# Turning the attention's output by transposing transfers in place of TensorE

## What is computed

```python
x = x + attention(group_norm(x))      # layer 0
x = x + factorised(group_norm(x))     # layer 1
# attention: f = Wq x + bq, g = Wk x + bk (32 channels each), h = Wv x + bv (256)
#   s = f^T g (4096 x 4096 an image); beta = softmax(s, axis=1); o = gamma * h beta
# factorised: y = relu(bn(w1 x + b1)) (32 channels); all 528 products y_i * y_j;
#   z = relu(bn(w2 products + b2)) (256)
```

## Time and profile before

| what | value |
|---|---|
| median of 3 runs | 2105.32 us (2105.01 to 2105.93) |
| the profiled execution, time and span | 2109.38 us, 2107.6 us |
| granted TensorE clock | full speed in every slice |
| DMA, mean share of the 16 engines | 66.6% for the one queue of SyncE |
| transposes by TensorE, `tps<-idn,ot` | 256 |

### The profile page before, as it was taken

The page is one execution under the profiler, slowest core; times in us unless marked ns, Lnnn a source line. Parts: engine busy times, 40 slices in busy tenths (PEclk is TensorE's granted clock), DMA queues, the critical chain, the costliest instruction groups (busy, mean ns, idle before and its releaser), DMA issues.

```text
span 2107.6 us, 48084 instructions
## 1 busy us (share of the span) xinstructions
PE 2056.0 (98%) x17334; PEld 1611.1 (76%) x17334; DVE 1656.5 (79%) x3617; ACT 1539.2 (73%) x2456; POOL 1479.8 (70%) x2110
## 2 busy tenths in 40 slices
PE   5899999999999999999999999999999999999999
PEld 3688888888877777777877777777787777777854
DVE  8788988778777877878768788777877768777767
ACT  5677777767776777778777787777777777777767
POOL 3265666667677777878768787777867767677766
PEclk9999999999999999999999999999999999999999
DMA  5165778776476788778478678887836767675632
GB/s 190 37 101 103 129 143 143 139 132 113 84 133 122 146 158 150 154 145 156 98 140 140 117 156 142 159 167 139 157 78 134 144 124 140 118 142 94 139 72 81
DMA packets 728269, 271.89 MB, mean 129 GB/s; under 512 B 674240, under 2 KB 681152, under 8 KB 728000
## 3 DMA queue, kind: packets, MB, share of 16 engines
q1 hardware_dynamic: 728032, 268.82, 66.6%
HBM read 77.07 MB, written 19.92 MB: 46 GB/s over the span
## 4 chain that ended last, share of the span: by engine, by line
PE 86%; DVE 5%; POOL 3%; ACT 2%; issue 2%; DMA 1%; SPq 0%; DVEq 0%; ACTq 0%; POOLq 0%
PE acc L1784 19%; PE acc L1772 19%; PE acc L1773 18%; PE tps L1577 5%; PE acc L1577 5%; PE sps L1597 4%; PE acc L1571 3%; PE tps L1648 3%; PE tps L1650 2%; PE acc L1648 1%; POOL kb L1162 1%; PE tps L1612 1%; DVE ks L863 1%; PE tps L1634 1%; POOL xl L1139 1%
## 5 line engine op out<-in xcount | busy, mean ns | idle before, releaser
L1162 POOL TENSOR_TENSOR kb<-ks,kb 128x512 f16<-128x512 f32 x630 | 760.3, 1211 | 412.1 <-DVE kb L891 315.6
L1772 PE MATMUL acc<-hth,kt 128*128 128x257 f16 x2520 | 587.2, 273 | 1.1 <-DMA kt<-kb 1.1
L1773 PE MATMUL acc<-htl,kt 128*128 128x256 f16 x2520 | 586.6, 273 | 0.0
L1333 ACT ACTIVATE ph<-sps,esc 128x512 f16<-128x512 f32 x394 | 269.5, 684 | 339.7 <-PE sps L1597 329.8
L1345 ACT ACTIVATE ks<-ks,kbias,esc 128x512 f32<-128x512 f32 x630 | 498.9, 805 | 0.0
L1784 PE MATMUL acc<-hth,kt 128*128 128x257 f16 x2520 | 385.8, 274 | 0.0
L863 DVE TENSOR_SCALAR_CACHE_REDUCE ks<-acc 128x512 f32<-128x512 f32 x378 | 259.2, 686 | 158.8 <-PE acc L1577 157.0
L1772 PE MATMUL acc<-hth,ph 128*128 128x257 f16 x1576 | 367.3, 274 | 0.0
L1773 PE MATMUL acc<-htl,ph 128*128 128x256 f16 x1576 | 366.9, 273 | 0.0
L1784 PEld LDWEIGHTS acc<-hth,kt 128*128 128x128 f16 x2520 | 247.7, 98 | 100.6
L1772 PEld LDWEIGHTS acc<-hth,kt 128*128 128x128 f16 x2520 | 247.0, 98 | 41.6 <-issue 6.2
(11 more groups left out here) (254 smaller groups left out, 3444.7 us busy)
## 6 DMA issues: line engine op xcount, KB each, us to landing
rt<-turned SPq DMA_DIRECT2D x96, 256.0 KB, 4.9
xt<-x SPq DMA_DIRECT2D x46, 512.0 KB, 4.5
xb<-x SPq DMA_DIRECT2D x32, 512.0 KB, 4.7
out<-zt SPq DMA_DIRECT2D x45, 256.0 KB, 2.7
kt<-kb SPq DMA_TRANSPOSE x630, 3.2
yb<-turned SPq DMA_DIRECT2D x36, 128.0 KB, 2.6
rt<-turned SPq DMA_DIRECT2D x72, 64.0 KB, 2.2
turned<-yb SPq DMA_DIRECT2D x12, 256.0 KB, 2.5
```

Of the source, the lines that this page charges most:

```text
L1162: tt(kb[:, m % KB_RING, 1], ks[:, m % KS_RING], kb[:, m % KB_RING, 0], ALU.subtract).then_inc(kl_ok, 1)
L1333: A(ph[:, v % SLOTS], sps[v % 2][:], ACT.Exp, scale=esc[:]).then_inc(ph_ok, 1)
L1772: mm(bank[:, 0:C + 1], high[:, q], hth[:, c * QT + q], start=(s8 == 0 and q == 0), stop=False)
L1773: mm(bank[:, 0:C], high[:, q], htl[:, c * QT + q], start=False, stop=False)
```

## The change

The outputs of the chunks J = 0 to 6 of each image (28 of 32, `by_transfer`) are turned by a transposing transfer. ScalarE divides into a float16 high half (`oth[:, k, 0]`, the same memory as `ot`); VectorE takes the low half from PSUM at s8 = 5 of the next tile (`output_low`); SyncE turns both halves of one tile into a new buffer `od` in one transfer (`turn_output`, s8 = 7, 128 x 512 float16). In the next chunk VectorE adds the high half and then the low half, each times the output scale, to x (`finish_turned`, four instructions of 128 x 512 at t = 9, 10, 12 and 14), and takes the statistics at t = 16 and 17 (`own_stats`). TensorE's transposes at t = 4 and 7 are gone, and the waits that stood with them are at t = 9; the last chunk of an image is turned by TensorE as before. The ring of x has 13 slots in place of 14, which gives the room for `od`, so that seven more x chunks pass through `xt`. The order of the value chunks, and the steps of four of them and of three statistics, are moved.

```diff
-XR = 14
+XR = 13
+        od = sb("od", [P, QT, 2 * H2, P], f16)
+        oth = ot[:].rearrange("p t c -> p (t c)").bitcast(f16).rearrange("p (t e c) -> p t e c", t=QT, e=2)
-        VORD = (4, 0, 5, 1, 6, 2, 3, 7)
+        VORD = (4, 0, 5, 3, 6, 1, 2, 7)
-        LATER_STATS = ((2, 27), (3, 2), (3, 9), (3, 18), (3, 25), (4, 2), (4, 9), (4, 18), (4, 25), (5, 2), (5, 9), (5, 18),
+        LATER_STATS = ((2, 27), (3, 2), (3, 11), (3, 18), (3, 25), (4, 2), (4, 11), (4, 18), (4, 25), (5, 2), (5, 11), (5, 18),
                        (6, 22), (6, 29), (7, 4), (7, 11))
-        V_EARLY = (12, 15, 18, 21)
+        V_EARLY = (11, 15, 19, 26)
         def in_place(b, c):
-            return b == 0 or (c < XR - NCH if b == 1 else c < 4)
+            return b == 0 or (c < XR - NCH if b == 1 else c < 3)
+        def by_transfer(G):
+            return G % NCH != NCH - 1
+        def transfers_before(G):
+            return G - G // NCH
+        def tiles_lowered(tile):
+            return QT * transfers_before(tile // QT) + (tile % QT + 1 if by_transfer(tile // QT) else 0)
...
+            def turn_output(tile):
+                G, k = divmod(tile, QT)
+                sp.wait_ge(ot_low, tiles_lowered(tile))
+                if transfers_before(G):
+                    sp.wait_ge(own_ok, 2 * H2 * transfers_before(G))
+                sp.dma_start_transpose(od[:, k], oth[:, k].rearrange("p e c -> p (e c)")).then_inc(od_in, 16)
...
+                        if t % NCH == 7 and tile and by_transfer((tile - 1) // QT) and (J or t >= NCH):
+                            turn_output(tile - 1)
...
+            def output_low(tile):
+                k = tile % QT
+                dve.wait_ge(ot_act, tile + 1)
+                V.scalar_tensor_tensor(oth[:, k, 1], acc[tile % 2][:, 0:C], rinv[:, k:k + 1], oth[:, k, 0],
+                                       ALU.mult, ALU.subtract).then_inc(ot_low, 1)
+            def finish_turned(G, e, h):
+                b, J = divmod(G, NCH)
+                if e == h == 0:
+                    dve.wait_ge(od_in, 16 * QT * (transfers_before(G) + 1))
+                    dve.wait_ge(bv_ok, G + 1)
+                if e:
+                    dve.wait_ge(own_ok, 2 * H2 * transfers_before(G) + h + 1)
+                own = xb[:, x_slot(b, J), h].rearrange("p (t q) -> p t q", t=QT)
+                V.scalar_tensor_tensor(own, od[:, :, H2 * e + h], vout[:, h:h + 1], own,
+                                       ALU.mult, ALU.add).then_inc(own_ok, 1)
+            def own_stats(G, h):
+                b, J = divmod(G, NCH)
+                dve.wait_ge(own_ok, 2 * H2 * transfers_before(G) + H2 + h + 1)
+                V.bn_stats(bst[:, h, J], xb[:, x_slot(b, J), h])
...
+                        if s8 == 5 and tile and by_transfer((tile - 1) // QT) and (J or t >= NCH):
+                            output_low(tile - 1)
...
-                        if J and t in (5, 8):
-                            finish(G - 1, (t - 5) // 3, 1)
-                        if J and t in (6, 11):
-                            second_stats(G - 1, (t - 6) // 5, 1)
+                        if J and t in (9, 10, 12, 14):
+                            finish_turned(G - 1, *((0, 0), (0, 1), (1, 0), (1, 1))[(9, 10, 12, 14).index(t)])
+                        if J and t in (16, 17):
+                            own_stats(G - 1, t - 16)
...
+                if transfers_before(G):
+                    act.wait_ge(od_in, 16 * QT * transfers_before(G))
+                if by_transfer(G):
+                    A(oth[:, k, 0], acc[tile % 2][:, 0:C], ACT.Copy, scale=rinv[:, k:k + 1]).then_inc(ot_act, 1)
+                    return
...
-                        if J and t in (4, 7):
-                            if t == 4 and b and n >= 1:
+                        if J and t == 9:
+                            if b and n >= 1:
                                 pe.wait_ge(y_ok, y_made(n - 1))
...
-                            transposed(G - 1, (t - 4) // 3, 1)
...
                         elif s8 == 0 and tile >= 2:
                             pe.wait_ge(ot_act, tile - 1)
+                            if by_transfer((tile - 2) // QT):
+                                pe.wait_ge(ot_low, tiles_lowered(tile - 2))
```

More of the change, by code:

```diff
@@ L203, in build @@
         rinv_ok = sem("rinv_ok")
-        ot_act = sem("ot_act")
+        ot_act, ot_low, od_in, own_ok = sem("ot_act"), sem("ot_low"), sem("od_in"), sem("own_ok")
         y_mm, y_ok = sem("y_mm"), sem("y_ok")
@@ L1051, in attend @@
                             normed(("qk", b + 1, 2 * (J - 2)))
-                        if b < LASTB and J == NCH - 1 and t in (13, 16, 19, 22):
-                            normed(("v", b + 1, VORD[(13, 16, 19, 22).index(t)]))
+                        if b < LASTB and J == NCH - 1 and t - 1 in V_EARLY:
+                            normed(("v", b + 1, VORD[V_EARLY.index(t - 1)]))
             project()
@@ L1225, in _ @@
                             low(("qk", b + 1, 2 * (J - 3) + 1))
-                        if t in (14, 17, 20, 23) and b < LASTB and J == NCH - 1:
-                            low(("v", b + 1, VORD[(14, 17, 20, 23).index(t)]))
+                        if t - 2 in V_EARLY and b < LASTB and J == NCH - 1:
+                            low(("v", b + 1, VORD[V_EARLY.index(t - 2)]))
                         if t == 20 and b and 1 <= n < SHARED - 1:
@@ L1349, in divide @@
                 act.wait_ge(rinv_ok, tile + 1)
-                k = tile % QT
+                k, G = tile % QT, tile // QT
+                if transfers_before(G):
[3 more added lines that the diff above has]
+                    return
                 A(ot[:, k], acc[tile % 2][:, 0:C], ACT.Copy, scale=rinv[:, k:k + 1]).then_inc(ot_act, 1)
@@ L1456, in attend @@
                             high(("qk", b + 1, 2 * (J - 2)))
-                        if b < LASTB and J == NCH - 1 and t in (12, 15, 18, 21):
-                            high(("v", b + 1, VORD[(12, 15, 18, 21).index(t)]))
+                        if b < LASTB and J == NCH - 1 and t in V_EARLY:
+                            high(("v", b + 1, VORD[V_EARLY.index(t)]))
             act.wait_ge(set_dve, mark["scaled_qkv"])
@@ L1747, in attend @@
                             rest_of_z(n - 2)
-                        if J and t in (4, 7):
-                            if t == 4 and b and n >= 1:
+                        if J and t == 9:
+                            if b and n >= 1:
                                 pe.wait_ge(y_ok, y_made(n - 1))
-                            if t == 4 and b and n >= 2:
+                            if b and n >= 2:
                                 pe.wait_ge(z_ok, 2 * (n - 1))
-                            if t == 4 and b < LASTB and 4 <= J <= 7:
+                            if b < LASTB and 4 <= J <= 7:
                                 pe.wait_ge(qk_lo, qk_made(b + 1, 2 * (J - 4)))
-                            if (b, J, t) == (0, 2, 4):
+                            if (b, J) == (0, 2):
                                 pe.wait_ge(set_dve, mark["part1"])
-                            transposed(G - 1, (t - 4) // 3, 1)
                         if kept(u):
```

## The result

The changed kernel takes 2168.98 us (2166.16 to 2170.22), the kernel before 2105.62 (2105.01 to 2109.87) beside it: a ratio of 1.0294, with a 95% interval of 1.0278 to 1.0311. It is 63 us slower. I had forecast 9 us slower, with a range up to 2132. Every ratio here has an interval of some 0.15% (3 us) on either side, so a difference between two changed kernels is known to about 4 us.

A forecast was written before the change was run, and what follows sets the result against it. TensorE was taken to bound the kernel (busy 2056.0 of 2107.6 us). 2109.4 - 24.6 (transposes) + 36.9 (VectorE's backlog) - 3 (relief) = 2118.7; with the runs' median 4.1 lower, 2115 us, range 2088 to 2132.

The forecast's parts named there:

- VectorE's backlog: VectorE running behind TensorE, mainly t = 9 to 18; added work makes TensorE wait: 36.9 us, less 3 us relief elsewhere.
- Image 0: Its chunks lose most: 2.3 us each for J = 3 to 6, 3.6 each for J = 1, 2 and 7.
- One sign of being wrong: VectorE waiting for od at t = 9, which would point to the transfers; no size given.
- the transfer of t = 7: Turned output wanted at t = 9, some 4 us after issue, against 3.2 us to land: hidden, no cost.
- a rival, at 28 us and little chance: Transfers of t = 7 land late, VectorE stands at t = 9: 2143 us; 0.10 together with ports always meeting.
- the blocked instruction: Rival: finish_turned always meets GpSimd's SBUF reads, 1.18 us each: 2145 us; chance 0.10 together with late transfers.
- the price of finish_turned: Four per chunk at t = 9 to 14, 0.89 us each, from similar rows' mean of 968 ns; bounds 0.60 and 1.18.
- "never blocked": Rival: finish_turned mostly falls between GpSimd's instructions, 0.60 us each, backlog costs 15.6 us: 2093 us; chance 0.34.
- the free backlog: About 2.05 us that VectorE may lag without cost to TensorE, from chunks 25 and 27 at t = 5 to 9.
- The transfers: 112 transposing transfers of 128 KB on SyncE's queue: 0 to 8 us, taken as 0; kt has five steps of cover.
- The ring: x in 13 slots, seven more loads through xt: zero, upper bound 5 us if one is caught behind a waiting queue.
- TensorE's gain: 56 groups of four transposes leave TensorE at 0.44 us each, all on the path: 24.6 us saved.

The follow-up runs named there:

- e1: Kernel before with only the 13 slots, the value chunks' new order and steps and the moved statistics; TensorE turns all outputs: 2114.49 us, ratio 1.0040.
- e14: As e13, but VectorE does not wait for the turned output at t = 9: 2111.75 us, ratio 1.0021.
- e13: Changed kernel with each finish_turned replaced by a statistics instruction on the same half of x (one SBUF input), same waits and places: 2130.69 us, ratio 1.0116.
- e9: e1 plus 112 transposing transfers of 128 KB from a constant tile that nobody reads, with ScalarE's wait for them: 2127.21 us, ratio 1.0093.
- e2: Kernel before with only one of four transposes of each half done for chunks J = 0 to 6; waits, finish and statistics stay: 2094.13 us, ratio 0.9943.
- e10: Changed kernel without finish_turned; SyncE waits for the transfers of the chunk before in place of VectorE: 2103.17 us, ratio 0.9983.
- e5: Kernel before, with finish of chunks J = 0 to 6 reading the unturned output in SBUF in place of PSUM: 2116.06 us, ratio 1.0042.
- e3: Changed kernel with the transfer of a chunk's first tile issued at t = 23 in place of 15: 2182.13 us, ratio 1.0360.
- e11: As e8, but the first tile's transfer issued at t = 26 in place of 23: 2139.92 us, ratio 1.0149.
- e8: As e3, but finish_turned at t = 18, 19, 20 and 21 and the statistics at 22 and 24: 2138.91 us, ratio 1.0154.

## Why the prediction was wrong, point by point

**Right.** VectorE's backlog turns the change's sign; the stretch is t = 9 to 18; finish_turned is blocked at its second SBUF input (1034 ns, against 968 from the model's row); `output_low` (477 ns a record) and the unchanged division (467 ns) were as assumed. Image 0 was of the right order: the windows of chunks 2 and 4 grew by 1.7 and 2.8, where I had 3.6 and 2.3, and its seven chunks by 23.4, of which 7.1 are e1's, where I had 20.0. One sign of being wrong that I had named came true, VectorE waiting for `od` at t = 9.

**The first step that failed: that the transfer of t = 7 is "hidden".** I compared a landing of 3.2 us with about 4 us until VectorE wants the output. Both sides were off. These 28 transfers landed 2.4 to 5.3 us after issue, median 3.7, though all 112 have a median of 2.6. And VectorE came to its instruction 1.6 to 4.9 us after the issue, median 2.8, since SyncE, in its own order, came to them between 2.0 us before and 3.9 us after TensorE's piece of t = 7. The twenty waits are up to 2.4 us long, and each stops VectorE's queue in front of its crowded steps. I had priced this as a rival, at 28 us and little chance; it measured 19 (e14). It was no rival to the blocked instruction: both happened, and a forecast that lets each happen alone has no place for their sum. By my own figures that sum was 2115 + 30 + 28 = 2173, against 2169 measured. The range ended at 2132 because it left out the tenth that I gave to the two.

**The mis-sized term: the price of finish_turned.** The sum had 36.9 us for VectorE's backlog; the stretch from t = 9 to 18 lost 69.9, of which 7.1 are e1's. My sum took 4 x 0.89 us a chunk against a floor of 0.60, which is 21 us of the span between "mean" and "never blocked" (36.9 less 15.6). Measured between blocked and not: 38 (e13). The record was 7% longer than the row that I took, and that it came so near is partly luck: two of the four were blocked more (1266 ns) and two less (802). The rest is the free backlog: chunk 13 grew by 4.3 and chunk 27 by 2.1 where I had 1.15 and 0.3, and the images 1 to 3 together by 46.6 (without chunk 31) where I had 16.9. For them I had counted the saving of t = 5 to 8 as credit, had taken 2.05 us of backlog as free from two chunks alone, and had spread the four instructions over t = 9 to 14; but the first two come at 1.3 us each right at the start, beside `value_bias` and `product_low`, and behind the wait for od. How much of the gap each of these makes was not parted.

**Set to zero, and not zero.** The transfers: 12.7 (e9), above the 8 us that I gave as their bound, because I looked at TensorE's use of kt and not at the reuse of `kb`, put ScalarE's wait for the transfers at nothing (9.8 us of waits in e9, 12.2 in the changed kernel), and took half the bytes for perhaps half the issue. The ring: 8.5 (e1), above the 5 us of its bound, 5.0 of it close to the case that I had named, one load that comes too late, though not behind a waiting queue: the steps of the statistics had been called harmless without a look at who uses `xt` next.

**TensorE's gain:** 24.6 from the row, of which e2 shows two thirds coming through while the rest of VectorE's work stands. Where VectorE's backlog allows it, the row is right: 0.44 us a group in most chunks of the changed kernel, 18.9 us of it before t = 9. From e9 to e10, which has no `finish` but `output_low`, the time falls by 24.0 us, and VectorE's busy time is the same in both (1656.5 and 1659.2 us).

With the measured sizes the sum reads 2105.6 + 8.5 + 12.7 - 24.0 + 8.6 + 18.9 + 38.3 = 2168.6, against 2169.0. That it closes is no test, since every term is the difference of two neighbouring kernels (before, e1, e9, e10, e14, e13, changed); it says where the 63 us stand. The -24.0 also holds `finish`, which e10 leaves out, and `output_low`, which it has and e9 has not.

**Open.** That it is GpSimd which blocks `finish_turned` rests on the lengths with and without its work beside them, and on e5 and e13, which change the inputs; no run took GpSimd's work away or moved `finish_turned` off `value_bias` alone. How much of e3's loss is the pair of transfers and how much the delay of the first tile was not told apart, nor why e11, which parts them, gained nothing over e8. `output_low` was in all of the kernels with transfers that are read; e10's trace shows that it costs little with `finish_turned` gone, and not what it costs beside it.

## What to carry to other kernels

When an engine is full in a stretch, price a moved operation by what its operands do there: an input that goes from PSUM to SBUF makes the instruction longer where another engine reads beside it (here, beside GpSimd, by 0.13 us on the mean in e5, 0.3 us in the changed kernel, 0.5 at its steps t = 9 and 10). Look which of that engine's instructions stands in the same step. A transfer that an in-order queue waits for needs its late landings and a late issue covered, not the median landing, and a further transfer on the same queue is paid by whoever reuses the source buffers of the others. If two rivals do not exclude each other, put their sum into the range.

## What was unexpected of the hardware

A transposing transfer of 128 KB (128 x 512 float16) holds SyncE's queue for 1.19 us at least, one of 256 KB (128 x 1024) for 1.23: the issue hardly got cheaper with the bytes. Landing did in the changed kernel (2.6 us median, 3.3 for the larger), but not in e9 (3.1 and 3.2), and the last of a chunk's four had a median of 3.7.

The two engines delayed each other: with `finish_turned` beside it, GpSimd's `value_bias` went from a median of 693 ns to 1112.
